# Row maxima turned by VectorE instead of TensorE, computed 52 units ahead, split on GpSimd, with the next keys loaded in two halves

## The reference

```python
Q, K, V = (proj(Wq), proj(Wk), proj(Wv))          # einsum('oc,bct->bto') over x
att = einsum('bhqd,bhkd->bhqk', Q, K) / sqrt(Dh) + b[0]
att = softmax(att * m + (1 - m) * -1e30)           # m: mask over the keys
y   = einsum('bhqk,bhkd->bhqd', att, V)            # back to (B, C, T)
q   = clip(round(y / in_scale), -128, 127)         # in_scale: |y|max of a row / 127
ffn = einsum('bsk,nk->bsn', q, weight) * in_scale * w_scale + bias   # as float16
out = x + ffn
```

## Time and profile before

| | |
|---|---|
| median of the runs | 2439.57 us |
| profiled execution, its own time | 2440.84 us |
| its span (first to last instruction) | 2439.0 us |
| granted TensorE clock, mean | 0.993 of full speed |
| busy: PE / PEld / DVE / ACT / POOL | 98 / 55 / 64 / 55 / 69 % of the span |

### The profile page before, as it was taken

One profiled execution on the slowest core, in us unless ns is written; L12 is line 12 of the kernel. 1 busy time (PEld: TensorE's weight loads), 2 busy tenths in 40 slices (PEclk: granted clock), 3 DMA queues, 4 the chain that ended last, 5 costly groups with the idle time before them and its releaser, 6 DMA issues.

```text
span 2439.0 us, 37390 instructions
## 1 busy us (share of the span) xinstructions
PE 2387.2 (98%) x12376; PEld 1341.0 (55%) x12376; DVE 1560.4 (64%) x1683; ACT 1346.3 (55%) x2536; POOL 1672.1 (69%) x677
## 2 busy tenths in 40 slices
PE   8999999997999999999999999999999999999996
PEld 7888888884444444444444444444444444444442
DVE  3311111145777777777777777777777877777771
ACT  3222222214666666666666666666666666666664
POOL 3322223414778888888877888888788888887777
PEclk9999999998999999999999999999999999999999
DMA  6655555365677776777677777666776667776751
GB/s 243 252 200 199 214 193 195 147 211 126 147 160 160 157 157 147 157 159 159 151 159 159 156 160 156 157 151 150 160 160 155 155 150 160 160 155 154 157 111 44
DMA packets 143498, 396.55 MB, mean 163 GB/s; under 512 B 14584, under 2 KB 50424, under 8 KB 127296
## 3 DMA queue, kind: packets, MB, share of 16 engines
q0 software_dynamic: 18144, 132.13, 27.4%
q10 hardware_dynamic: 49312, 130.80, 22.8%
q1 hardware_dynamic: 75968, 132.74, 14.9%
HBM read 161.51 MB, written 100.93 MB: 108 GB/s over the span
## 4 chain that ended last, share of the span: by engine, by line
PE 67%; DMA 4%; issue 2%; POOL 2%; DVE 2%; ACT 0%; SPq 0%; ACTq 0%; POOLq 0%; DVEq 0%
PE score L689 21%; PE pv L716 18%; PE ring L127 18%; PE ring L749 4%; DMA q_stack<-max_lo 4%; PE ring L726 2%; PE ring L729 2%; DVE neg_max L136 1%; PE ring L740 1%; POOL acc L988 1%; PE ring L734 0%; DMA probs<-probs 0%; POOL acc L1000 0%; ACT probs L798 0%; SPq L609 0%
## 5 line engine op out<-in xcount | busy, mean ns | idle before, releaser
L798 ACT ACTIVATE probs<-score 128x512 f32<-128x512 f32 x2048 | 1074.7, 604 | 576.4 <-PE score L689 559.5
L136 DVE TENSOR_REDUCE neg_max<-ring 128x1 f32<-128x1024 f32 x1024 | 1208.4, 1220 | 230.8 <-PE ring L127 219.1
L689 PE MATMUL score<-q_stack,k_stack 100*128 100x512 f32 x2048 | 875.8, 429 | 23.9 <-DMA q_stack<-max_lo 16.6
L988 POOL TENSOR_TENSOR acc<-acc,probs 128x2048 f32<-128x2048 f32 x189 | 867.1, 4588 | 26.6 <-DMA probs<-probs 11.9
L127 PE MATMUL ring<-k_stack,q_stack 98*128 98x512 f32 x2048 | 810.6, 396 | 0.3 <-DVE neg_max L136 0.2
L689 PEld LDWEIGHTS score<-q_stack,k_stack 100*128 100x128 f32 x2048 | 387.3, 189 | 504.0 <-ACT probs L798 358.2
L716 PE MATMUL pv<-probs,v_in 128*32 128x512 f32 x4096 | 546.1, 605 | 0.0
L127 PEld LDWEIGHTS ring<-k_stack,q_stack 98*128 98x128 f32 x2048 | 390.8, 191 | 66.6 <-DVE neg_max L136 0.8
L988 POOL TENSOR_TENSOR acc<-probs 128x2048 f32<-128x2048 f32 x63 | 288.8, 4584 | 100.8 <-DMA probs<-probs 100.8
L479 POOL TENSOR_TENSOR q_stack<-x_raw,k_stack 128x1024 fp32r<-128x1024 f32 x28 | 67.7, 2450 | 294.7 <-ACT k_stack L364 294.7
L972 POOL DMA_DIRECT2D probs<-probs x126 | 108.2, 859 | 175.4 <-PE pv L716 168.2
(11 more groups left out here) (95 smaller groups left out, 2026.6 us busy)
## 6 DMA issues: line engine op xcount, KB each, us to landing
probs<-probs POOLq DMA_DIRECT2D x126, 1024.0 KB, 8.0
k_stack<-qk_part ACTq DMA_DIRECT2D x93, 512.0 KB
q_stack<-qk_part ACTq DMA_DIRECT2D x183, 256.0 KB, 5.4
qk_part<-part_hi SPq DMA_DIRECT2D x64, 512.0 KB, 2.6
qk_part<-part_lo SPq DMA_DIRECT2D x64, 512.0 KB, 3.5
v_steps<-v_out SPq DMA_DIRECT2D x64, 256.0 KB, 2.2
res<-x ACTq DMA_DIRECT2D x32, 512.0 KB, 5.7
out<-res SPq DMA_DIRECT2D x64, 256.0 KB, 2.1
```

What stands on the lines that cost most here:

```text
L136: nc.vector.tensor_reduce(neg_max[:, pair // CHUNK, pair % CHUNK:pair % CHUNK + 1], ring[:, :], AX_X, ALU.max, negate=True).then_inc(neg_m ...
L689: pe.matmul(score[score_bank(t)][:, :], k_stack[par][0:ROWS, h, kt * P:(kt + 1) * P], q_stack[par][0:ROWS, half, h, :], start=True, stop=T ...
L798: nc.scalar.activation(probs[:, kt, h, :], score[score_bank(t)][:, :], ACT.Exp).then_inc(exp_done, 1)
L988: nc.gpsimd.tensor_tensor(acc[:, half, :, :], first, probs[:, tile, :, :], ALU.add).then_inc(acc_done, 1)
```

## The change

- `OWN` goes from 20 to 12: pair 0 of the next step starts at unit 12, chunk 0 is complete after unit 43 (`MAXIMA_0`) and chunk 1 after unit 11 (`MAXIMA_1`). The tail of `project` computes 26 pairs of step 0 instead of 22: two among the projections, two behind them.
- TensorE no longer transposes the maxima. ScalarE copies the high part of `neg_max` (128 x 16) at unit 14 or 46, GpSimd subtracts the low part between its two `begin_pair`, VectorE transposes both at once in blocks of 32 x 32 at unit 17 or 49, and SP stores them with four DMAs of 32 partitions x 128 bytes instead of two of 16 x 512 bytes.
- The keys come as six DMAs of 256 KB. The first half of step s+2 is issued at units 58 to 60 of step s, the second half of s+1 at units 0 to 2, and the mask rows at 0 and 1 instead of 4 and 5.

The new `turn_max` is VectorE's, the new `low_max` GpSimd's.

```diff
-LOADS_K, LOADS_Q = 16 * 5, 16 * 3
+LOADS_K, LOADS_Q = 16 * 8, 16 * 3
-OWN = 20
+OWN = 12
 EARLY = (UNITS - OWN) // 2
+MAXIMA_1, MAXIMA_0 = OWN - 1, OWN + UNITS // 2 - 1
...
+def load_k(eng, qk_d, k_stack, s, par, half, k, loaded):
     part = (2, 3, 2)[k]
+    keys = slice(half * N, (half + 1) * N)
+    rows = qk_d[part][bass.ds(s * P, P), keys].rearrange("(h r) t -> r h t", h=GH)
+    eng.dma_start(k_stack[par][k * DH:(k + 1) * DH, :, keys].bitcast(F32), rows).then_inc(loaded[par], 16)
...
+                    for pair in range(TT * 3 * CT // 4, EARLY):
+                        pe.wait_ge(neg_max_done, pair - 1)
+                        for half in range(2):
+                            row_max(pe, ring[pair % 2], q_stack, k_stack, 0, pair, half, rowmax_done)
...
-        max_hi = sb("max_hi", [CHUNK, 2, P], F32R)
-        max_lo = sb("max_lo", [CHUNK, 2, P], F32R)
-        ident = sb("ident", [P, P], F32)
+        max_parts = sb("max_parts", [P, 2, 2, CHUNK], F32R)
+        max_turned = sb("max_turned", [P, 2, 2 * CHUNK], F32)
...
             def store_max(par, chunk):
-                for part, rows in ((0, max_hi), (1, max_lo)):
-                    dst = q_stack[par][ROW_MAX + part:ROW_MAX + part + 1, chunk, :, :]
-                    sp.dma_start(dst.bitcast(F32), rows[:, chunk, :].bitcast(F32)).then_inc(max_rows[chunk], 16)
+                rows = q_stack[par][ROW_MAX:ROW_MAX + 2, chunk, :, :].rearrange("r h (a g j) -> r h a g j", g=P // DH, j=DH)
+                for g in range(P // DH):
+                    sp.dma_start(rows[:, :, :, g, :].bitcast(F32), max_turned[g * DH:(g + 1) * DH, chunk, :]).then_inc(max_rows[chunk], 16)
...
-            def turn_max(s, chunk, buf):
-                pe.wait_ge(neg_max_done, PAIRS * s + CHUNK * (chunk + 1))
-                pe.transpose(buf[0:CHUNK, N:N + P], neg_max[:, chunk, :], ident[:, :]).then_inc(maxT_done, 1)
...
+            def high_max(s, chunk):
+                act.wait_ge(neg_max_done, PAIRS * s + CHUNK * (chunk + 1))
+                wait(act, max_turn_done, 2 * (s - 1) + chunk + 1)
+                nc.scalar.activation(max_parts[:, chunk, 0, :], neg_max[:, chunk, :], ACT.Copy).then_inc(max_hi_done, 1)
...
                 if ahead and t < 3:
                     if t == 0:
                         wait(act, score_done, UNITS * s)
-                    load_k(act, qk_d, k_stack, s + 1, 1 - par, t, k_loaded)
-                if ahead and t in (4, 5):
-                    load_bias(act, bias_d, k_stack, s + 1, 1 - par, t - 4, k_loaded)
+                    load_k(act, qk_d, k_stack, s + 1, 1 - par, 1, t, k_loaded)
+                if ahead and t < 2:
+                    load_bias(act, bias_d, k_stack, s + 1, 1 - par, t, k_loaded)
...
+                if ahead and t in (58, 59, 60) and not (isinstance(s, int) and s + 2 >= STEPS):
+                    act.wait_ge(score_done, UNITS * s + UNITS - 2 * GH * 2)
+                    load_k(act, qk_d, k_stack, s + 2, par, 0, t - 58, k_loaded)
...
+            def turn_max(s, chunk):
+                dve.wait_ge(max_lo_done, 2 * s + chunk + 1)
+                wait(dve, max_rows[chunk], MAX_ROWS * s)
+                nc.vector.transpose(max_turned[:, chunk, :],
+                                    max_parts[:, chunk, :, :].rearrange("p a b -> p (a b)").bitcast(F32)).then_inc(max_turn_done, 1)
...
+            def low_max(s, chunk):
+                pool.wait_ge(max_hi_done, 2 * s + chunk + 1)
+                nc.gpsimd.tensor_tensor(max_parts[:, chunk, 1, :], neg_max[:, chunk, :],
+                                        max_parts[:, chunk, 0, :].bitcast(F32), ALU.subtract).then_inc(max_lo_done, 1)
...
                 if main:
-                    for i in range(2):
-                        begin_pair(s, 0, i)
+                    begin_pair(s, 0, 0)
+                    low_max(s, 1)
+                    begin_pair(s, 0, 1)
                     add(s, 0, 0)
```

More of the change, by code:

```diff
@@ L266, in _ @@
             for k in range(3):
-                load_k(sp, qk_d, k_stack, 0, 0, k, k_loaded)
+                for half in range(2):
+                    load_k(sp, qk_d, k_stack, 0, 0, half, k, k_loaded)
             for part in range(2):
@@ L556, in attend @@
         max_lo_done = sem("max_lo_done")
+        max_turn_done = sem("max_turn_done")
         recip_done = sem("recip_done")
@@ L571, in attend @@
         res_done = sem("res_done")
[L573 removed]
+        MAX_ROWS = 16 * P // DH
         def halves_before(s, half):
@@ L659, in wait_ring @@
                 elif t in (SUMS_1, SUMS_0):
-                    wait(pe, sums_out, 2 * s + (t == SUMS_0))
-                    if not isinstance(s, int) or s + (t == SUMS_0) < STEPS:
-                        pe.wait_ge(max_lo_done, 2 * s + (2 if t == SUMS_1 else 3))
+                    pe.wait_ge(sums_out, 2 * s + (t == SUMS_0))
                 elif t == TURN_Q:
@@ L671, in take_ring @@
                     pe.wait_ge(neg_max_done, EARLY)
-                    wait(pe, max_lo_done, s + 1)
                 else:
@@ L762, in step @@
                     use = ("extra", t)
[L763 to L774 removed]
+                    if t == SUMS_1 and prev:
+                        sum_rows(s - 1, 1, take_ring(s, par, use))
+                    if t == SUMS_0 and main:
+                        sum_rows(s, 0, take_ring(s, par, use))
                     if t == TURN_Q and prev:
@@ L853, in step @@
                         take_y(s - 1, 1)
-                    if t == SUMS_1 and main:
-                        high_max(s, 1, ring_of(par, ("extra", SUMS_1)))
+                    if t == MAXIMA_1 + 3 and main:
+                        high_max(s, 1)
                     if t == 35 and main:
@@ L861, in step @@
                         make_ints(s - 1, (t - 41) // 2)
-                    if t == SUMS_0 and ahead:
-                        high_max(s + 1, 0, ring_of(par, ("extra", SUMS_0)))
-            act.wait_ge(const_set, 5)
+                    if t == MAXIMA_0 + 3 and ahead:
+                        high_max(s + 1, 0)
+            act.wait_ge(const_set, 4)
             act.wait_ge(stack_set, 4)
@@ L929, in step @@
                         reduce_max(nc, dve, ring_of(par, ("max", t)), neg_max, own, pair, rowmax_done, neg_max_done)
-                    if t == SUMS_1 and main:
-                        low_max(s, 1, ring_of(par, ("extra", SUMS_1)))
+                    if t == MAXIMA_1 + 6 and main:
+                        turn_max(s, 1)
+                    if t == MAXIMA_0 + 6 and ahead:
+                        turn_max(s + 1, 0)
                     if t == 19 and prev:
@@ L946, in step @@
                             scale_product(s - 1, half, ring_of(par, ("extra", FFN)))
-                    if t == SUMS_0 and ahead:
-                        low_max(s + 1, 0, ring_of(par, ("extra", SUMS_0)))
                     if t == SUMS_0 and main:
@@ L1032, in step @@
                 if main and ahead:
-                    for i in range(2):
-                        begin_pair(s, 1, i)
+                    begin_pair(s, 1, 0)
+                if ahead:
+                    low_max(s + 1, 0)
+                if main and ahead:
+                    begin_pair(s, 1, 1)
                 if main and not ahead:
```

46 lines of the change are left out of this document (9 added, 37 removed).

## The result

The changed kernel took 2454.11 us (median of 5 runs, 2453.24 to 2461.86) against 2440.74 us for the kernel before on the same chip (5 runs, 2439.23 to 2442.15). The ratio is 1.0066, with a 95% interval from 1.0048 to 1.0084: slower by 13.4 us, where the prediction had 17 us faster. The time lies outside the predicted range as well.

What follows compares the result with a forecast made beforehand. TensorE, busy 98%, bounds the kernel, with 0.50 us of each 57.59 us step waiting in units 24 to 35. Terms: -32.2 + 2.4 + 12.9 = -16.9, so 2423.9 us by the profile, 2423 by the median; range 2409 to 2437.

Steps and rivals of the forecast that it cites:

- Turns off TensorE: At units 23 and 55, removing 63 transposes of the maxima from TensorE's path at 0.21 us each saves 13.2 us.
- Mask rows: In units 4 to 7, mask-row issues at units 0 and 1 delay exponential 4; TensorE waits 0.43 us a step, 12.9 us.
- Rival B: Units 4 to 7: the moved mask rows cost nothing and the groups stay at 3.05; time 2410 us, chance 0.17.
- The start: Before and in step 0: four more products 1.0, longer chain to the first score 0.9, keys 0.5; together 2.4 us lost.
- rival E: At unit 12 the keys arrive late; with 0.5 us of wait per step the time is 2438 us; chance 0.07.
- GpSimd's link: Units 17 and 49: VectorE waits for GpSimd's subtraction, which costs nothing until it is 1.6 us late.
- rival D: Units 17 and 49: GpSimd's late subtraction holds VectorE, making the kernel slower; 2465 us at 3 us late, chance 0.07.
- So unit 32 should no longer wait: Chunk 1's store starts about 5 us earlier against 1.2 to 2.7 for two more issues; most of 13.5 us saved.
- rival C: Units 24 to 35: the waits stay, from GpSimd's accumulating DMAs or SP's four slow issues; 2436.5 us, chance 0.17.
- SP's issues no longer meet ScalarE's: Units 24 to 26: ScalarE's slow DMA issues go; part of the 0.45 us taken back in each of steps 1 to 30.
- Step 0 and the last step: Step 0's unit 32 wait and slow clock go, 2.24 and 1.5 us; the last step gives back 1.13 and 0.7.
- the light groups of the last step: Units 12 to 19 lose their maximum products; 0.35 us saved for each of two groups, 0.7 in all.

Runs made afterwards that it cites:

- e1: The changed kernel with the two mask-row loads moved back behind units 4 and 5; 2513.91 us, ratio 1.0289 to the kernel before.
- e5: The changed kernel with mask rows back behind units 4 and 5 and a constant tile stored by two DMAs of 16 x 512 B; 2419.58 us, ratio 0.9908.
- e8: e7 with SP instead of ScalarE issuing the mask rows and the second half of the queries; 2414.44 us, ratio 0.9887 to the kernel before.
- e4: The changed kernel with chunk 1's high part copied earlier and VectorE, not GpSimd, subtracting, then transposing right behind unit 11's maximum; 2450.97 us, ratio 1.0038.
- e6: The changed kernel storing a constant tile, not the maxima, with four DMAs of 8 pieces of 512 B; 2435.32 us, ratio 0.9972.
- e2: The changed kernel storing a constant tile, not the maxima, with two DMAs of 16 pieces of 512 B; 2429.66 us, ratio 0.995.
- e7: The changed kernel with chunk 1's high part copied at unit 12, GpSimd subtracting before its other work, and the turn at unit 15; 2435.85 us, ratio 0.9971.
- e3: The changed kernel with GpSimd's accumulating DMAs cut from 1 MB to 64 columns of one head; 2416.8 us, ratio 0.9899.

## Why the prediction was wrong

**Turns off TensorE: right mechanism, the term too small.** Forecast 4.91 for the groups with the sums, measured 4.78: 0.35 and not 0.21 for each, 22 us and not 13.2. I had read the turn's cost as the distance to the next start, 0.21. The turn also starts later behind its `pv` (1.00 us, 1426.09 to 1427.09) than a sum does now (0.89):

```profile
1436.49 1.06 PE L718 MATMUL pv<-probs,v_in 128*32 128x512 f32 x8
1437.38 1.04 PE L728 MATMUL ring<-probs,ones 128*32 128x512 f32 x8
```

**Mask rows: right.** 0.41 a step against 0.43, by the place and mechanism named. Rival B is out (e1, e5, e8 get 3.05 to 3.07 with the rows elsewhere).

**The start: about right as a sum, in part by luck.** The first score comes 2.5 us later, against 1.9. But TensorE reaches the idle time ahead of it 2.8 us later (559.71 against 556.89), where the four products had 1.0, and the chain from there takes 14.3 us against 14.6, where the forecast had 0.9 more. Over the kernels measured here TensorE got there between 558.5 and 561.2, so part of the 2.8 is chance. Keys at unit 12 of step 0 were 1.15 late, against 0.5. In steady steps no unit 12 waits: rival E is out.

**GpSimd's link: right but for step 1.** In the steps 2 to 30 VectorE's transposition never waited for GpSimd: rival D is out there, and e4 shows what it would have looked like. In step 1 GpSimd was behind with its adds. The transposition waited 1.19 us, and the maximum product behind it 0.54:

```profile
645.23 0.21 DVE L874 STREAM_TRANSPOSE max_turned<-max_parts 128x32 f32<-128x32 f32 x1 [1.19 <-POOL max_parts L964]
```

**The failed step is "So unit 32 should no longer wait".** Its first two terms were in bounds: 4.46 us earlier instead of 5, 2.71 for two more issues against 1.2 to 2.7. What it left out is the landing, taken silently at the old 6.88 us; it became 8.89. With 5 - 2.7 = 2.3 us of lead expected at the bad end, 2.0 of landing and 0.35 of a shorter group with the sums used all of it.

The semaphores in the traces show what the landing goes by. Means of steps 2 to 30, in us from the start of the `pv` of unit 23; the second accumulating DMA is issued at about -1.33 in all of these runs:

| | store: last issue | store landed | second accumulating DMA landed | unit 32 could start |
|---|---|---|---|---|
| before | +2.53 | +9.45 | +8.77 | +9.47 |
| after | +0.76 | +9.69 | +8.80 | +9.20 |
| e1 | +0.79 | +11.27 | +9.26 | +9.27 |
| e6 (four long) | +1.10 | +8.97 | +9.01 | +9.28 |
| e2 (two long) | -1.94 | +4.52 | +8.89 | +9.19 |
| e7 | -2.29 | +3.48 | +9.05 | +9.18 |
| e4 | -4.26 | +1.77 | +7.60 | +8.85 |

Where the last issue comes behind the second accumulating DMA, the store lands within 1 us of that DMA (2 us in e1), in the kernel before as well. Where it comes ahead of it, the store lands 4 us and more earlier. So the earlier start gained nothing as long as the last issue was behind that DMA, and two more slow issues kept it there. The two waits of e8 fit: there the last issue was at -1.63 and -1.36 and the store landed at +10.6 and +10.8, against +4.3 on the mean. The line is not sharp, though: in step 1 of e7 the last issue was 0.3 us ahead and the store still landed late, at +11.3, and in the last step of e2 it was 0.1 us behind and landed 3.3 us ahead of that DMA.

Of the 5.2 us between e2 and after, four DMAs in place of two make 4.45 (e6), and the short pieces 0.7. These 0.7 tipped a store that e6 lands 0.3 us in time. e2 and e6 (form), e3 (traffic) and e4 and e7 (place) each take the wait away or nearly so. That the place in the order is what counts is read from these runs; two DMAs with short pieces were never run.

This is rival C with a chance of 0.17, and even C had the waits stay at 0.50, where they became 1.05 (0.30 in units 28 to 31, 0.72 in 32 to 35, 0.03 behind them). By the profile's own time the forecast was 2423.9 and after took 2460.5, 36.6 more. Of these, 22 lie in steps 2 to 30: 29 x 1.0 = 29 for waits that should have gone and grew instead, less 29 x 0.28 = 8 for the turns, and the rest in roundings. The other 15 lie in the first steps and the last, below.

The Trainium skill, "DMA: Bandwidth & Descriptors", section Specifications, asks for pieces of at least 512 B. The runs agree in direction: with four DMAs each, 128 B against 512 B is 57.90 against 57.34 us a step. They also bound it, since in e3 the same short pieces cost nothing. Nor was a piece slow by itself: by the DMA records one of 128 B took 0.015 us in after, one of 512 B 0.041 in e6. The 128 pieces of a store come to 2.0 us, spread over more than one DMA engine; the rest of the 8.9 us was waiting. I had cited the rule and then given it no term in the sum.

The two forms differ in one more thing: each short DMA ends in two writes to its semaphore, each long one in 8 (e6) or 16 (before and e2). I take that as the number of DMA engines that carry it, so that the expectation of e2, two pieces for each of 16 engines, would be wrong. No run tells the length of the pieces from the number of engines.

**A second failed step: "SP's issues no longer meet ScalarE's".** True and without effect. e3 shows the accumulating DMAs to be what slows them. The loss in units 28 to 31 that I counted as saved, 0.24 in before and 0.30 in after, was never SP's.

**Step 0 and the last step: right at their places, lost behind them.** Units 32 to 39 of step 0 are 3.9 us shorter, against 3.7. And the light groups of the last step, units 12 to 19, take 2.70 each and not 3.05, the 0.7 of the forecast. But unit 32 of step 1, behind the late link above, waits 4.14 us, and the last one, whose 1.13 I took back, waits 1.93. Behind that wait the clock stays down. TensorE's timeline and a window of the last step:

```profile
2398.81 2.06 PE L691 MATMUL score<-q_stack,k_stack 100*128 100x512 f32 x4 [1.93 <-DMA q_stack<-max_turned]
```

```profile
2404.00:2405.00 1.00, 1.00 (x6) 0.34 (x9) 0.00 (x0) 1.00 (x3) 1.00 (x1) 0.50 0.00 0
```

The granted clock is at 0.50, the 1.2 GHz level, for three groups of 4.15 us each, units 36 to 47, which took 2.69, 3.36 and 3.17 in before. Like before's, they have no maximum products. In e3, without the wait, the stretch from the `ffn` of step 30 to that of step 31 takes 53.68 us, in before 56.26 and in after 60.71. The 2.6 us between e3 and before are 0.7 for the light groups, 0.7 for two turns and 1.2 for the wait of before, so these terms were sized rightly. The five runs of after differ by up to 8.6 us; that single waits like these make the difference is not shown, since only one of them has a profile.

**Left open:** why the landing of e1 grew by another 1.55 us; why the store of step 1 takes 12.16 us to land behind its last issue; how two DMAs with short pieces would do; and whether the 0.7 us are the short pieces' or the fewer engines'.

## What to carry to other kernels

Price a moved transfer from issue to landing at its new place and in its new form; the earlier start is only the first of three terms. Look at the last issue, and whether it goes out ahead of the large transfer beside it or behind. A wait at one fixed point swallows what is saved ahead of it, and behind several of the waits of about 2 us seen here (e1, the last step of after) the next groups ran at half clock. Where a DMA issue sits between two instructions of an engine that others wait for, give it to a queue with nobody behind.

## What the hardware showed that I had not expected

- A VectorE subtraction of 128x16 from two tiles in SBUF took 1.69 us beside GpSimd's add. So it went in all 31 such subtractions of chunk 1 in e4: they took 1.67 to 3.34 us, and each ended 0.03 to 0.04 us behind the end of an add of GpSimd. The 33 others took 0.16 to 0.18. GpSimd's own 128x16 subtraction takes 0.24 between two other instructions (e7); the 0.52 in after begins while the DMA issue ahead of it still runs, and 0.26 of it lie behind that.
- The issue of a 256 KB load on ScalarE's queue took 0.32 us, and one of the store on SP's 0.61. In the stretches shown both took 1.2 to 1.3 while a 1 MB accumulating DMA was under way; with these DMAs cut to 64 columns the longest of SP's 256 is 0.73.
